# Score matmuls of two heads on 64 rows each, stacked inside SBUF: a transformer block of 2048 tokens on one core

## The reference

```python
q, k, v = x @ Wq.T + bq, x @ Wk.T + bk, x @ Wv.T + bv      # per head of 8
scores  = where(causal, q @ k.T / sqrt(8), -inf)
att     = softmax(scores) @ v
x = layernorm(x + att @ Wo.T + bo)
# top-1 of 8 experts by sigmoid(router), plus a shared expert, FF 256
x = layernorm(x + moe(x) + shared(x))
```

## Time and profile before

| | |
|---|---|
| median of 3 runs | 608.11 us (606.51 to 609.79) |
| profiled execution | 612.24 us |
| its span, first to last instruction | 610.5 us |
| mean granted clock of PE | 0.947 of 2.4 GHz |
| DMA | 25.62 MB, mean 42 GB/s |

### The profile page before, as it was taken

One profiled execution on the slowest core, in us unless ns is written; L12 is line 12 of the kernel. 1 busy time (PEld: TensorE's weight loads), 2 busy tenths in 40 slices (PEclk: granted clock), 3 DMA queues, 4 the chain that ended last, 5 costly groups with the idle time before them and its releaser, 6 DMA issues.

```text
span 610.5 us, 10445 instructions
## 1 busy us (share of the span) xinstructions
PE 550.3 (90%) x3497; PEld 233.8 (38%) x3497; DVE 456.6 (75%) x765; ACT 356.8 (58%) x803; POOL 150.7 (25%) x267
## 2 busy tenths in 40 slices
PE   5539599999999999999999999999999899998980
PEld 3224234434333334333333333333434225664460
DVE  5728378999989988888888878888872515777684
ACT  3003355746567766877777776767778884331350
POOL 5651123130211202111001101101003157215644
PEclk9655789999999999999999999999999999999995
DMA  5736300036200045100000000000000111211233
GB/s 125 170 59 112 47 1 2 28 96 115 55 1 28 1 119 115 31 2 18 12 1 28 1 1 28 2 1 2 1 1 20 35 32 48 51 37 52 43 68 90
DMA packets 22909, 25.62 MB, mean 42 GB/s; under 512 B 2987, under 2 KB 21363, under 8 KB 22275
## 3 DMA queue, kind: packets, MB, share of 16 engines
q1 hardware_dynamic: 20896, 21.67, 15.2%
q0 software_dynamic: 1536, 3.15, 2.9%
q10 hardware_dynamic: 424, 0.13, 0.1%
HBM read 17.44 MB, written 7.21 MB: 40 GB/s over the span
## 4 chain that ended last, share of the span: by engine, by line
PE 73%; DVE 10%; DMA 6%; issue 5%; POOL 3%; ACT 2%; SPq 0%; POOLq 0%; DVEq 0%; ACTq 0%
PE out_ps L1271 21%; PE score_ps L1230 19%; PE ring_ps L1254 19%; DVE part_max L966 5%; DMA q_stack<-max_rows 3%; PE score_ps L1360 3%; PE score_ps L1233 2%; PE ring_ps L1377 1%; PE ring_ps L1280 1%; POOL k_stack L789 1%; PE score_ps L1312 1%; POOL qk_parts L776 1%; PE score_ps L1254 1%; PE ring_ps L1195 1%; PE ring_ps L1241 1%
## 5 line engine op out<-in xcount | busy, mean ns | idle before, releaser
L966 DVE TENSOR_REDUCE part_max<-score_ps 128x2 f32<-128x1024 f32 (+3 forms) x320 | 327.7, 1062 | 75.3 <-PE score_ps L1233 45.8
L843 ACT ACTIVATE probs<-ring_ps 128x512 f32<-128x512 f32 (+3 forms) x611 | 285.1, 537 | 123.9 <-PE ring_ps L1254 121.8
L1230 PE MATMUL score_ps<-k_stack,q_stack 96*128 96x512 bf16 (+3 forms) x640 | 182.3, 364 | 19.0 <-issue 10.5
L1254 PE MATMUL ring_ps<-q_stack,k_stack 96*128 96x512 bf16 (+3 forms) x611 | 172.9, 353 | 7.4 <-DMA q_stack<-max_rows 5.7
L1271 PE MATMUL out_ps<-probs,v_aug 128*32 128x512 f32 (+3 forms) x1280 | 150.7, 543 | 4.3 <-POOL probs L710 3.8
L1230 PEld LDWEIGHTS score_ps<-k_stack,q_stack 96*128 96x128 bf16 x640 | 60.5, 101 | 107.9 <-DVE part_max L966 39.2
L1254 PEld LDWEIGHTS ring_ps<-q_stack,k_stack 96*128 96x128 bf16 x611 | 52.1, 98 | 120.3 <-ACT probs L843 69.4
L710 POOL TENSOR_SCALAR_AFFINE_SELECT probs<-probs 128x512 f32<-128x512 f32 x64 | 40.6, 634 | 165.2 <-ACT probs L843 165.0
L1233 PE MATMUL score_ps<-mask_qk,ident_bf 128*128 128x128 bf16 x256 | 57.1, 241 | 0.0
L1271 PEld LDWEIGHTS out_ps<-probs,v_aug 128*32 128x32 f32 x1280 | 25.4, 108 | 49.6 <-issue 23.8
L721 POOL CAST max_parts<-row_max 128x16 bf16<-128x16 f32 x48 | 9.4, 196 | 117.7 <-DVE row_max L974 115.6
(11 more groups left out here) (179 smaller groups left out, 417.6 us busy)
## 6 DMA issues: line engine op xcount, KB each, us to landing
q_stack<-parts_dram SPq DMA_DIRECT2D x9, 384.0 KB
k_stack<-parts_dram SPq DMA_DIRECT2D x27, 128.0 KB
parts_dram<-qk_parts SPq DMA_DIRECT2D x8, 384.0 KB, 2.7
sorted_dram<-q_stack SPq DMA_DIRECT2D x30, 64.0 KB, 1.5
x_sb<-in_L_attn_x_dram SPq DMA_DIRECT2D x4, 256.0 KB, 5.2
w_gu<-n_L_ffn_expert_gate_dram SPq DMA_DIRECT2D x8, 128.0 KB, 2.2
w_gu<-in_L_ffn_expert_up_dram SPq DMA_DIRECT2D x8, 128.0 KB, 2.4
wd<-n_L_ffn_expert_down_dram SPq DMA_DIRECT2D x8, 128.0 KB, 2.3
```

What stands on the lines that cost most here:

```text
L843: act.activation(probs[:, n % RING, 0:w], bank(it)[:, 0:w], ACT.Exp, scale=SCALE).then_inc(probs_ready, 1)
L966: dve.tensor_reduce(out=part_max[:, s % 2, t, 2 * hp:2 * hp + 2, c], in_=score_ps[:, m % 2, :, 0:w], axis=AX.X, op=ALU.max).then_inc(score ...
L1230: last = mm(score_ps[:, m % 2, i, 0:w], q_stack[0:KROWS, B % 2, h, t * P:(t + 1) * P], k_stack[0:KROWS, c, h, 0:w], start=True, stop=c < B)
L1254: mm(bank(it)[:, 0:w], k_stack[0:KROWS, j // TPB, h, j % TPB * P:(j % TPB + 1) * P], q_stack[0:KROWS, B % 2, h, skip:BLK], start=True, sto ...
```

## The change

Three things.

1. The stacks have 64 rows per head. Eight of the nine products (all but low times low) fill 8 x 8 = 64 rows, MAIN; a second tile of 64 rows, REST, has the ninth product on every eighth row, the maxima on three rows, else zeros (q) or -1 (k). Head h stands on rows 0 to 63 for h under 8, on rows 64 to 127 otherwise. A score job multiplies MAIN alone, for one head of each half; a probability item makes two heads at once (640 tiles, 320 items), each as MAIN plus REST added up in PSUM. The mask matmul of a job becomes four of 64 rows. The three bfloat16 parts are kept in another order, and the heads of `out_ps` too.
2. A probability item takes two banks at once (of three; of five after the last job); PE waits for the second before the second MAIN. The planner gets new costs for it, and charges 107 ns for each change between kinds of array tiles.
3. The stacks are copied inside SBUF, without DRAM: per block and side one DMA of 128 KB for each product (8) and one for the lows, each to every eighth partition, so 16 rows. Block 0 is no longer cut by heads. Maxima go in two DMAs.

The core of the diff:

```diff
+SWITCH = 107
-BACKGROUND_UNIT = 3
-VALUE_LAG = 3
...
-            for i in range(4):
+            for i in range(2):
...
-            return max(clock["tensor"], ring[turns % 3], in_place)
+            return max(clock["tensor"], ring[turns % 3], ring[(turns + 1) % 3], in_place)
...
-            clock["tensor"] += 0.84 * w + 8 + 107 * (c == B)
+            clock["tensor"] += 0.42 * w + 85 * (c == B)
...
-            clock["tensor"] += 0.42 * w + 3
-            clock["scalar"] = max(clock["scalar"], clock["tensor"] + LATENCY) + 0.83 * w + 52
-            ring[turns % 3] = clock["scalar"] + 60
-            turns += 1
+            clock["tensor"] += 0.84 * w
+            for _ in range(2):
+                clock["scalar"] = max(clock["scalar"], clock["tensor"] + LATENCY) + 0.83 * w + 52
+                ring[turns % 3] = clock["scalar"] + 60
+                turns += 1
...
-            clock["tensor"] += 1.83 * (BLK - P * max(0, item[4] - TPB * item[2]))
+            clock["tensor"] += 1.67 * (BLK - P * max(0, item[4] - TPB * item[2]))
...
+    HALF = H // 2
+    PRODUCTS = [(a, r) for a in reversed(range(PARTS)) for r in reversed(range(PARTS)) if a or r]
+    HALVES = (slice(0, 64), slice(64, P))
+    MAIN, REST = 0, 1
...
+        elif it[0] == "probs":
+            choices = list(combinations((4, 5, 6) + ((0, 1) if late else ()), 2))
...
+            mine = sorted(mine, key=lambda b: given.get(b, -1))
+            for i, b in enumerate(mine):
+                unit = ("probs", 2 * it[1] + i)
+                bank_of[unit] = b
+                held_before[unit] = [holder[b]] if b in holder else []
...
-            sp.dma_start(bias_qk[:, 1:2], bk.rearrange("(h d) -> d h", d=HD),
-                         allow_slow_non_contiguous=True).then_inc(bias_qk_loaded, 16)
+            for half in HALVES:
+                sp.dma_start(bias_qk[half, 1:2], bk[half].rearrange("(h d) -> d h", d=HD),
+                            allow_slow_non_contiguous=True).then_inc(bias_qk_loaded, 16)
...
+            def stack(side, b, part):
+                to = (q_stack, k_stack)[side]
+                at = b % 2 if side == 0 else b
+                parts = qk_parts[:, side, b % 2, part, :]
...
+                if side == 0 and b >= 2:
                     sp.wait_ge(exp_in_ready, units_before[b - 1])
...
+                for p, product in enumerate(PRODUCTS):
+                    if product[side] == part:
+                        sp.dma_start(to[p:P:HD, at, MAIN, :, :], parts).then_inc((q_stacked, k_stacked)[side][b], 16)
+                if part == 0:
+                    sp.wait_ge((q_filled, k_filled)[side], (min(b, 1), b)[side] + 1)
+                    sp.dma_start(to[0:P:HD, at, REST, :, :], parts).then_inc((q_lows_stacked, k_lows_stacked)[side][b], 16)
+
+            def stack_block(b):
+                for part in reversed(range(PARTS)):
+                    for side in range(2):
+                        stack(side, b, part)
...
-                    sp.dma_start(q_stack[STACK:STACK + PARTS, B % 2, 4 * g:4 * g + 4, :],
-                                 max_rows[:, s % 2, :]).then_inc(max_rows_placed[s % 2], 16)
+                    for x in range(2):
+                        sp.dma_start(q_stack[64 * x + 1:64 * x + 1 + PARTS, B % 2, REST, 2 * g:2 * g + 2, :],
+                                     max_rows[2 * PARTS * x:2 * PARTS * (x + 1), s % 2, :]).then_inc(max_rows_placed[s % 2], 16)
...
-                minus_ones = k_stack[64:96, b, :, :].bitcast(F32)
-                pool.memset(minus_ones, MINUS_ONES).then_inc(k_filled, 1)
+                pool.memset(k_stack[:, b, REST, :, :].bitcast(F32), MINUS_ONES).then_inc(k_filled, 1)
...
-                    for i in range(2):
-                        h = 4 * g + 2 * hp + i
-                        last = mm(score_ps[:, m % 2, i, 0:w], q_stack[0:KROWS, B % 2, h, t * P:(t + 1) * P],
-                                  k_stack[0:KROWS, c, h, 0:w], start=True, stop=c < B)
-                        if c == B:
-                            last = mm(score_ps[:, m % 2, i, w - P:w], ident_bf[:, :], mask_qk[:, :],
-                                      start=False, stop=True)
+                    for x, half in enumerate(HALVES):
+                        hh = 2 * g + hp
+                        last = mm(score_ps[:, m % 2, x, 0:w], q_stack[half, B % 2, MAIN, hh, t * P:(t + 1) * P],
+                                  k_stack[half, c, MAIN, hh, 0:w], start=True, stop=c < B)
+                    if c == B:
+                        for y, skip in enumerate((0, 64)):
+                            for x, half in enumerate(HALVES):
+                                at = 64 * (x - y)
+                                last = mm(score_ps[:, m % 2, x, w - P + skip:w], ident_wide[half, 64 + at:64 + at + P],
+                                          mask_wide[half, at + skip:at + P], start=False, stop=y == 1)
...
-                    mm(bank(it)[:, 0:w], k_stack[0:KROWS, j // TPB, h, j % TPB * P:(j % TPB + 1) * P],
-                       q_stack[0:KROWS, B % 2, h, skip:BLK], start=True, stop=True).then_inc(exp_in_ready, 1)
+                    for rows in (MAIN, REST):
+                        for x, half in enumerate(HALVES):
+                            unit = ("probs", 2 * n + x)
+                            if rows == MAIN:
+                                wait_bank(unit)
+                            last = mm(bank(unit)[:, 0:w], k_stack[half, j // TPB, rows, hh, keys],
+                                      q_stack[half, B % 2, rows, hh, skip:BLK], start=rows == MAIN, stop=rows == REST)
+                            if rows == REST:
+                                last.then_inc(exp_in_ready, 1)
...
-                        last = turn(bank(it)[:, g * P:(g + 1) * P], oT[:, B % 2, g, t * P:(t + 1) * P], ident[:, :])
+                        last = turn(by_head[:, :, g, :], oT[:, B % 2, g, t * P:(t + 1) * P], ident[:, :])
```

More of the change, by code:

```diff
@@ L2 @@
 from contextlib import ExitStack
+from itertools import combinations
 import concourse.bass as bass
@@ L75, in make_plan @@
     main, finish = [], []
-    unit = quad = before = 0
+    pair = quad = before = 0
     value = None
@@ L84, in make_plan @@
         for ql, (g, j) in enumerate(quads):
-            for i in range(4):
[L86 to L89, removed]
+            for i in range(2):
+                due = sum(d <= begin + LEAD[B] + (ql + i / 2) / len(quads) * (end - begin) for d in done[1:])
+                main.append((("probs", pair, B, g, j, i), due))
+                pair += 1
+                if i == 1 and ql > START[B] and (ql - START[B]) % SPREAD[B] == 0 and background:
                     main.append((background.pop(0), due))
-                if i == VALUE_LAG and value is not None:
+                if i == 1 and value is not None:
                     main.append((value, due))
@@ L106, in make_plan, with switch @@
     slots, ring, exp_done, max_ready, max_placed = [0.0, 0.0], [0.0] * 3, {}, {}, {}
-    plan, job, turns = [], 0, 0
+    plan, job, turns, rows = [], 0, 0, P
+    def switch(kind):
+        nonlocal rows
+        last, rows = rows, 64 if kind in ("scores", "probs") else 32 if kind == "values" else P
+        return SWITCH if rows != last else 0
     def start_of(item):
@@ L128, in put @@
         clock["tensor"] = start_of(item)
+        if kind in costs or kind in ("scores", "probs", "values"):
+            clock["tensor"] += switch(kind)
         plan.append(item)
@@ L217, in block_kernel, with head @@
     SCALE = float(HD) ** -0.5
-    STACK = PARTS * PARTS * HD
-    KROWS = 96
+    HALF = H // 2
+    PRODUCTS = [(a, r) for a in reversed(range(PARTS)) for r in reversed(range(PARTS)) if a or r]
+    HALVES = (slice(0, 64), slice(64, P))
+    MAIN, REST = 0, 1
     VC = HD + 1
-    assert D == P and H * HD == D and STACK + PARTS <= KROWS
+    assert D == P and H * HD == D and len(PRODUCTS) == HD and HD * HD == 64
+    def head(g, i):
+        return 2 * g + i // 2 + HALF * (i % 2)
     plan, tail = make_plan(NB, G)
-    n_units = sum(1 for i in plan if i[0] == "probs")
+    n_units = 2 * sum(1 for i in plan if i[0] == "probs")
     def experts(w):
@@ L538, in block_kernel @@
         out_tiles = out.rearrange("a (n p) d -> p (a n) d", p=P)
-        STACKED = 16
-        CLEARED = 16
-        units_before = {B: sum(1 for it in plan if it[0] == "probs" and it[2] < B) for B in range(NB + 1)}
+        STACKED = 16 * len(PRODUCTS)
+        units_before = {B: sum(2 for it in plan if it[0] == "probs" and it[2] < B) for B in range(NB + 1)}
         def last_quad(s):
@@ L813, in _ @@
             for i in range(2):
-                act.activation(wT[:, i, :].rearrange("p (d h) -> p d h", d=HD),
-                               score_ps[:, 1, 0, i * D:(i + 1) * D].rearrange("p (h d) -> p d h", d=HD), ACT.Copy).then_inc(w_kept, 1)
+                for x in range(2):
+                    half = slice(i * D + 64 * x, i * D + 64 * (x + 1))
```

(3 more changed lines are left out.)

178 lines of the change are left out of this document (79 added, 99 removed).

## The result

The changed kernel takes 597.99 us (median of 4 runs, 596.98 to 598.45) against 607.62 for the kernel before on the same chip: a ratio of 0.985, with an interval of 0.9808 to 0.9893. It is faster by 1.5%; forecast were 4.7%. The profiled execution of after took 598.1 us around a span of 596.4; the profiled one of before took 612.24 around 610.5.

A forecast was written before the change was run, and what follows sets the result against it. PE was taken to bound 75 to 455 us, DVE close behind, and waits for stacks and maxima the opening. Profiled 612.2 less 14 (opening) less 15 (that stretch) gave 583, scaled 579; range 545 to 608.

The forecast's parts named there:

- Opening: Stacks copied without DRAM: group 1's tiles at 59 us instead of 73.43, 14 us less (7 to 20).
- two ends: First score in the opening: at 18 us by SP's issue, 28 to 30 by the transfer rate; 24 taken.
- Row overlap: Score matmuls: two heads on the row halves stream fully together, one step of 0.217 us a job instead of two.
- (b): Rival, chance 0.14: row overlap incomplete, a step of two takes 0.28 us; 22 us more, 601 scaled.
- (d): Rival, chance 0.08: row halves run one after another, probability matmuls double; 717 us scaled.
- The chain of the pairs: Probability tiles: second pair waits for the first pair's first exp, 1.29 us; full-width quad 2.81 us against 2.83.
- the sum for 75 to 455 us: Attention proper, 133 quads: 2 full-width, 9 narrow, 10 masks, 4 idle, less 8 and 2: 15 us less.
- Steps in the quads: Within the sum for 75 to 455 us: 2 us taken off for output copies on ACT delaying an exp.
- rival (c): Chance 0.16: score jobs miss the gap, each returning 0.217 us to PE's chain; 608 with one of two missed, 637 both.
- Narrow quads: Quads 384, 256 and 128 columns wide, 13 each: 0.12, 0.23 and 0.35 us less, 9 us together.
- Rival (a): Chance 0.16: the order fills the gap and DVE binds; 75 to 455 us takes 43 less, 551 scaled.

The follow-up runs named there:

- the last run: The changed kernel with values in halves only in the full-width quads before the last score, whole elsewhere: 584.03 us, ratio 0.9636.

## Why the prediction was right in sign and wrong in size

- **Opening, -14 forecast; -20.8 in these traces, some -16.5 by the medians.** The mechanism held: both waits went. That the first score came at 22.23, near the 24 forecast, is partly luck, as 24 was a middle of two ends and neither was so: SP's issue took 0.64 us a copy, not the 0.33 of before's loads, and ran without a pause from 9.31 to 20.94, and the data moved at 200 GB/s, not 137. The second queue brought the first score only 0.9 forward, so the transfers were as near a limit. The first tile came at 42.06 for 46, as a group's jobs took 6.6 and not 7.4; from there to group 1's tiles it was 13.2 us for 13. Another 2.7 us were gone by quad 5. There the granted clock differs: before, where PE had stood for 5.68 us, it was 0.50 (1.2 GHz) until 80 us and 1.00 from 82 on; after, without that wait, 1.00 from 59 on.
- **Row overlap** was full (0.43 for two jobs): rivals (b) and (d) are out.
- **The chain of the pairs** was right to 0.02: 1.29 from pair to pair and 2.82 for 2.81. The Trainium skill, "TensorEngine Tiling (Array Packing)", section "PSUM Bottleneck", says that emptying PSUM does not get faster with the tiles and may become the limit. The trace agrees: by PE alone the scores were worth 56 us and they gave none, and half an exp took 0.21 us off a quad, though ACT, at 61%, is not full; here it is the time until a bank comes free that counts.
- **The step that failed** is the sum for 75 to 455 us, -15 forecast; quads 5 to 133 took 6.9 more. Its part for the full-width quads (2 for the chain, 10 for masks, 4 for idle time, less 8 and 2) says 6 gained in 94. By the table they lost 10.0 in 84. The old side of it was fair: plain full-width quads took 2.85 on average, and 31 of the 35 took 2.82 or more. The floor of 2.81 was right too. But the sum let every quad reach it, which takes all jobs in the gap and other steps at their old price. After the change 23 of the 35 lie at 2.82 and 12 above, 3.07 on average, nine of them with a job ahead of the first pair.
- **Jobs outside the gap**: in those 84 quads the starts show 23% of the jobs' columns ahead of the first pair or behind the second, where a job costs its 0.22 (3.04 for 2.82), some 8 us in all. That is rival (c) for a quarter of the jobs, though not for its reason: with half the maxima these quads stay at 3.04, so it is the order of the plan, and not VectorE, that puts the job there.
- **Steps in the quads** I had at nothing beyond the 2 us of output copies. One turn of 128 columns cost a quad 0.11 before (392.87 - 389.93 = 2.94 for 2.83) and 0.26 after (422.44 - 419.36 = 3.08 for 2.82), and the other turns and projections also 0.15 to 0.19 more: for 29 of them some 4.5 us. Before:

```profile
389.93 1.07 PE L1271 MATMUL out_ps<-probs,v_aug 128*32 128x512 f32 x8
...
392.66 0.28 PE L1285 MATMUL ring_ps<-ident,o_norm 128*128 128x128 f32 x1
392.87 1.07 PE L1271 MATMUL out_ps<-probs,v_aug 128*32 128x512 f32 x8
```

  These two are estimates from counts and prices in the traces, not runs; together they are some 12.5 of the 15.4 us between the 5.4 gained that the sum gives for 84 quads and the 10.0 lost. The rest stays open; the floor took some of it in quads that were light before, those with narrower values (2.49 for 2.27).
- **Narrow quads** gained 4.1 us in 27, against 9 in 39: two thirds of the forecast (6.2 for 27).
- **Rival (a)** did not come: VectorE was busy for 119.15 of 130 us and 204.48 of 245, and halving its work moved no plain quad of two jobs.

## What to carry to other kernels

Before crediting a saving to the engine that is full, work out the floor that the changed order has without it. Then ask of how many pieces the floor is the whole time: where the kernel's order is written ahead by a planner, as here, it can be counted before any run how much of the saved engine's work stands in the gaps, and what each step outside them costs in the new arrangement. Work that must lie between two waits pays when it is cut to fill both gaps evenly, and only where the wait is longer than the cut's own cost. For copies that spread rows over partitions, look at how the rows lie and at bytes per issue before blaming the memory behind them.

## What the runs showed of the hardware

- SP spent 0.63 to 0.65 us on issuing a copy inside SBUF, for 64 KB as for 128 KB. With 8 adjacent rows, where the data moved at 61 GB/s, the k copies took 16.75 / 9 = 1.86 us each.
- 128 KB copies to 16 rows that lie 8 apart moved 201 GB/s at a share of 0.72, at the pace of their issue; 64 KB copies to 8 rows that lie 8 apart 109 at 0.39; 128 KB copies to 8 adjacent rows 61 at 0.58.
- A second queue raised the engines' share from 0.72 to 1.13 and the rate only from 201 to 226 GB/s.
- Two matmuls on the two row halves cost as much as one, 0.22 us for 512 columns. Cutting the values' block in two cost 0.24 us a quad (not 0.17 a half, as the last run's expectation has it): twice 0.07 in the values (0.57 for 0.50) and 0.10 in the first pair (0.53 for 0.43).
